# Mixture-of-experts stage of a vision-tower kernel: the last seven expert slots at 64 rows, with the routing arithmetic rewritten for them

## The reference, cut to what matters

```python
def _L0_ffn_ref(x, norm_scale, w_router, w_up, w_down):
    xn = rms_norm(x, norm_scale)
    scores = jnp.einsum('bsd,ed->bse', xn, w_router)
    _, ids = jax.lax.top_k(scores, TOP_K)                 # TOP_K = 2 of 8
    probs = jax.nn.softmax(scores, axis=-1)
    c = jnp.take_along_axis(probs, ids, axis=-1)
    h = jnp.einsum('bsd,ehd->bseh', xn, w_up)             # 256 -> 1408, every expert
    val, gate = jnp.split(h, 2, axis=-1)
    h = val * jax.nn.silu(gate)                           # 704
    y = jnp.einsum('bseh,edh->bsed', h, w_down)           # 704 -> 256
    yk = jnp.take_along_axis(y, ids[..., None], axis=2)
    out = jnp.sum(yk * c[..., None], axis=2)
    return out + skip
```

## Time and profile before

| | us |
|---|---|
| median of three executions (lowest, highest) | 1308.99 (1300.41, 1309.66) |
| the profiled execution | 1306.81 |
| its span from first to last instruction | 1305.2 |
| PE busy (share of the span) | 1173.4 (90%) |
| PE weight loads | 940.5 (72%) |
| DVE, ACT, POOL busy | 761.0, 577.0, 458.2 |
| routing: from DVE's first instruction of it to the first turning of rows on PE | 230.24 to 249.21 |
| the slots: from there to the end of the last down product | 249.21 to about 562.6 |

### The profile page before, as it was taken

One profiled execution on the slowest core, in us unless ns is written; L12 is line 12 of the kernel. 1 busy time (PEld: TensorE's weight loads), 2 busy tenths in 40 slices (PEclk: granted clock), 3 DMA queues, 4 the chain that ended last, 5 costly groups with the idle time before them and its releaser, 6 DMA issues. The chain is left out here.

```text
span 1305.2 us, 26300 instructions
## 1 busy us (share of the span) xinstructions
PE 1173.4 (90%) x9755; PEld 940.5 (72%) x9755; DVE 761.0 (58%) x1709; ACT 577.0 (44%) x1514; POOL 458.2 (35%) x630
## 2 busy tenths in 40 slices
PE   6999998498999999998799999995899999879975
PEld 4666667498999999984477777774777777657643
DVE  4666666511111212157899999974677777432687
ACT  3445453111122111127888787851344444335455
POOL 0111111233233333234488787851122122020556
PEclk9999999599999999999999999997999999889985
DMA  4111100599788888639500000002000050027611
GB/s 145 46 46 37 49 10 18 207 350 387 296 325 322 316 314 327 235 114 270 158 1 1 1 2 1 1 1 89 9 10 10 14 198 2 2 68 281 201 46 66
DMA packets 82719, 162.34 MB, mean 124 GB/s; under 512 B 42976, under 2 KB 61536, under 8 KB 76576
## 3 DMA queue, kind: packets, MB, share of 16 engines
q1 hardware_dynamic: 63776, 114.44, 25.6%
q0 software_dynamic: 10224, 44.05, 8.7%
q10 hardware_dynamic: 8592, 2.16, 0.8%
HBM read 134.28 MB, written 26.35 MB: 123 GB/s over the span
## 5 line engine op out<-in xcount | busy, mean ns | idle before, releaser
L936 PE MATMUL banks<-rowsT,w_up 128*128 128x128 f32 x1716 | 201.7, 278 | 0.0
L936 PEld LDWEIGHTS banks<-rowsT,w_up 128*128 128x128 f32 x1716 | 198.6, 195 | 0.1
L1486 PEld LDWEIGHTS banks<-chain_q,ident 128*128 128x128 f32 x992 | 120.5, 188 | 29.2 <-issue 29.2
L1476 PE MATMUL banks<-xT_d,ident 128*128 128x512 f32 x256 | 123.6, 605 | 7.2 <-POOL xT_d L1934 3.7
L1934 POOL TENSOR_TENSOR xT_d<-kb,ys 128x1024 f32<-128x1024 f32 x64 | 123.7, 1932 | 7.1 <-ACT ys L1611 5.8
L1486 PE MATMUL banks<-chain_q,ident 128*128 128x128 f32 x992 | 120.9, 273 | 0.0
L1627 ACT ACTIVATE banks<-banks,rate 128x256 f32<-128x256 f32 x252 | 98.5, 448 | 41.9 <-DVE made L1835 39.4
L1105 DVE TENSOR_TENSOR hT<-banks,silu 64x128 f32<-64x128 f32 x39 | 11.0, 283 | 167.8 <-ACT silu L993 167.8
L950 PE MATMUL banks<-w_down,hT 128*128 128x256 f32 x468 | 107.5, 379 | 0.6 <-DVE res L1115 0.6
L950 PEld LDWEIGHTS banks<-w_down,hT 128*128 128x128 f32 x468 | 85.9, 190 | 11.0 <-issue 1.0
L878 POOL DMA_DIRECT2D w_down<-in_down_w x39 | 22.2, 570 | 189.5 <-PE banks L950 181.3
(11 more groups left out here) (332 smaller groups left out, 2409.1 us busy)
## 6 DMA issues: line engine op xcount, KB each, us to landing
w_up<-in_up_w SPq DMA_DIRECT2D x39, 1408.0 KB, 6.1
w_down<-in_down_w POOLq DMA_DIRECT2D x39, 768.0 KB, 5.3
inter<-res_x SPq DMA_DIRECT2D x16, 512.0 KB, 3.4
back<-inter SPq DMA_DIRECT2D x15, 512.0 KB, 3.8
patches<-in_patches SPq DMA_DIRECT2D x16, 384.0 KB, 3.3
f<-in_f SPq DMA_DIRECT2D x6, 1024.0 KB, 11.6
ys<-token_rows SPq DMA_DIRECT2D x16, 256.0 KB, 2.8
xn_rows<-xn_all SPq DMA_DIRECT2D x16, 128.0 KB, 1.7
```

Source lines behind the costliest of these rows:

```text
L936: ins = pe.matmul(out[:, m * P:(m + 1) * P], w[:, c, m * P:(m + 1) * P], x[:, c, :], start=(c == 0), stop=(c == 1))
L1476: pe.matmul(S[t % 2][:, halves[h], :, :], ident[:, :], outer[t % 2][:, halves[h], :, :], start=(t == 0), stop=True, skip_group_check=True) ...
L1486: ins = pe.matmul(o_sum[n % 2].rearrange("p (n s) -> p n s", s=2), ident[:, :], products[:, n % 2, :, k, :], start=(k == 0), stop=(k == HD ...
```

## The change

Slots 0 to 31 (`FULLS`) keep 128 rows; slots 32 to 38 have 64 (`used_rows`). An expert gets whole slots for its rows, and a remainder of 1 to 64 rows gets one half slot; where more than 32 whole ones are wanted, the rest stand in two half slots each (`odd_at`, `jump`, `upper`). The number of slots, and of loads of `w_up` and `w_down`, stays 39.

In a half slot the turning, the up products, the copies, the SiLU values and the multiplications take 64 rows. Each of the six down products is split into two column halves of `w_down`, which write partitions 0 to 63 and 64 to 127 of the result bank (`Y_HALF`), and DVE copies the result in two pieces.

In the routing, `choose_slots` and `name_rows` get more small instructions on DVE. `choose_experts` moves from DVE to POOL and is written as a chain of 13 instructions; POOL also makes `named` for the pairs (`name_pairs`). The fourth lot of `row_hot` moves to ACT: eight squares of the distance to the row, then one ReLU of 1 minus it. Behind the naming products PE issues eight dummy products (`keep_warm`).

The core of the diff:

```diff
+FULLS = 2 * T
+USED = FULLS + E - 1
...
+    Y_HALF = [banks[q * TOK:(q + 1) * TOK, 6, 0:P] for q in range(2)]
+    def used_rows(j):
+        return P if j < FULLS else TOK
...
-        pool.wait_ge(sem("tile_at"), 1)
+        pool.wait_ge(sem("h_padded"), 2)
+        pool.wait_ge(const_in, 16 * len(const))
+        choose_experts(pool)
+        name_pairs(pool)
         fetch_down(0)
         pool.wait_ge(sem("source"), 1)
         gather(0)
...
-                    ins = pe.matmul(out[:, m * P:(m + 1) * P], w[:, c, m * P:(m + 1) * P], x[:, c, :],
+                    ins = pe.matmul(out[:, m * P:m * P + n], w[:, c, m * P:(m + 1) * P], x[:, c, 0:n],
...
+            if j < FULLS:
+                for c in range(HIDC):
+                    ins = pe.matmul(Y, hT[j % 2][:, c, :], w_down[j % DEEP][:, c, :], start=(c == 0), stop=(c == FULL))
+            else:
+                for c in range(HIDC):
+                    for q in range(2):
+                        ins = pe.matmul(Y_HALF[q], hT[j % 2][:, c, 0:TOK], w_down[j % DEEP][:, c, q * P:(q + 1) * P],
+                                        start=(c == 0), stop=(c == FULL), skip_group_check=True)
...
-            if i % LOT == 0:
+            if i == ACT_LOT * LOT:
+                pe.wait_ge(sem("act_row_hot"), 1)
+            elif i % LOT == 0:
                 pe.wait_ge(sem("row_hot"), i // LOT + 1)
...
+        keep_warm(pe, banks[:, 2, 0:P], ident[:, :], 8)
...
+        act.wait_ge(sem("row"), 1)
+        for i in range(LOT):
+            ins = act.activation(distance[:, i, :], const["row_no"][:, :], ACT.Square, scale=-1.0,
+                                 bias=row[:, ACT_LOT * LOT + i:ACT_LOT * LOT + i + 1])
+        ins.then_inc(sem("distance"), 1)
...
+        act.activation(row_hot[:, ACT_LOT * LOT:PAIRS, :], distance[:, :, :], ACT.Relu, scale=-1.0, bias=1.0
+                       ).then_inc(sem("act_row_hot"), 1)
...
+    def choose_experts(pool):
+        pool.wait_ge(sem("odd_at"), 1)
...
+    def name_pairs(pool):
+        pool.wait_ge(sem("slot_hot"), 1)
+        pool.tensor_tensor(named[:, 0, :, :], slot_hot[:, :, :], bcast(const["pair_start"][:, :], 2, USED), ALU.mult
+                           ).then_inc(sem("pair_named"), 1)
...
-        for i in range(4):
+        for i in range(ACT_LOT):
...
+                dve.tensor_copy(res[j % KEPT][0:TOK, 0:P], Y_HALF[0])
+                dve.tensor_copy(res[j % KEPT][0:TOK, P:D], Y_HALF[1]).then_inc(sem("y_copied"), 1)
```

More of the change, by code:

```diff
@@ L833, in expert_layer @@
     per_tile = sb("per_tile", [P, E, T])
-    cmp = sb("cmp", [P, E, T])
-    need, ends, first = (sb(n, [P, E]) for n in ("need", "ends", "first"))
+    cmp = sb("cmp", [P, E, 2 * T])
+    need, ends, starts = (sb(n, [P, 2, E]) for n in ("need", "ends", "starts"))
+    odd_first, odd_at, ends_at, jump, limit, base = (sb(n, [P, E]) for n in (
+        "odd_first", "odd_at", "ends_at", "jump", "limit", "base"))
+    whole, odds_from = sb("whole", [P, 1]), sb("odds_from", [P, 1])
+    parts = sb("parts", [P, 2, E])
+    over = sb("over", [P, T, E])
+    upper = sb("upper", [P, PAIRS])
     where = sb("where", [P, T, E])
@@ L884, in gather @@
                 pool.wait_ge(sem("rowsT_made"), j - ROWS + 1)
+            n = used_rows(j)
             pool.indirect_dma_start(
[L886 to L887 removed]
+                out=rows[j % ROWS][0:n, :], out_offset=None, in_=xn_rows,
+                in_offset=bass.IndirectOffsetOnAxis(ap=source[0:n, j:j + 1].bitcast(U32), axis=0)
             ).then_inc(sem(f"rows{j % ROWS}"), 16)
@@ L948, in down @@
                 pe.wait_ge(sem("y_copied"), j)
-            for c in range(HIDC):
-                ins = pe.matmul(Y, hT[j % 2][:, c, :], w_down[j % DEEP][:, c, :], start=(c == 0), stop=(c == FULL))
+            if j < FULLS:
[6 more added lines that the diff above has]
+                                        start=(c == 0), stop=(c == FULL), skip_group_check=True)
             ins.then_inc(sem("y_made"), 1)
@@ L1065, in name_rows @@
                                             op1=ALU.subtract))
+        tally.settle()
+        tally.mark(dve.tensor_scalar(upper[:, :], row[:, :], float(TOK), float(TOK), ALU.is_ge, ALU.mult))
+        tally.settle()
+        tally.mark(dve.scalar_tensor_tensor(out=upper[:, :], in0=slot_at[:, :], scalar=float(FULLS * P), in1=upper[:, :],
+                                            op0=ALU.is_ge, op1=ALU.mult))
+        tally.settle()
+        tally.mark(dve.tensor_tensor(slot_at[:, :], slot_at[:, :], upper[:, :], ALU.add))
+        dve.tensor_tensor(row[:, :], row[:, :], upper[:, :], ALU.subtract).then_inc(sem("row"), 1)
+        tally.settle()
         dve.tensor_tensor(slot_hot[:, :, :], bcast(const["slot_start"][:, :], 1, PAIRS), bcast(slot_at[:, :], 2, USED),
                           ALU.is_equal).then_inc(sem("slot_hot"), 1)
-        choose_experts(dve, tally)
-        dve.wait_ge(sem("slot_hot"), 1)
-        dve.tensor_tensor(named[:, 0, :, :], slot_hot[:, :, :], bcast(const["pair_start"][:, :], 2, USED), ALU.mult
-                          ).then_inc(sem("pair_named"), 1)
-        for i in range(4):
+        dve.wait_ge(sem("row"), 1)
+        for i in range(ACT_LOT):
             at = slice(i * LOT, (i + 1) * LOT)
@@ L2908, in laid_out_more @@
     keep = np.tile(np.arange(T) > 0, E)
+    halves = np.arange(USED) + np.minimum(np.arange(USED), FULLS)
     return {
@@ L2921, in laid_out_more @@
         "keep": line(keep),
-        "keep_e": line(np.ones(E)),
-        "full": line(P * np.arange(T)),
+        "keep_e": line(np.arange(2 * E) % E > 0),
+        "full": line(TOK * np.arange(2 * T)),
         "row_no": line(np.arange(P)),
-        "slot_start": line(P * np.arange(USED)),
+        "slot_start": line(TOK * halves),
         "pair_start": line(P * np.arange(2 * T)),
```

120 lines of the change are left out of this document (80 added, 40 removed).

## The result

The changed kernel takes 1315.32 us (median of 13 runs, 1308.43 to 1328.48), the kernel before 1308.99 (13 runs). The ratio is 1.0062, with an interval of 1.0035 to 1.0089: slower by 0.6%, some 8 us (5 to 12 by the interval; the two medians lie 6.3 us apart), where 1307.5 and no change were forecast. It lies 1.3 us above the range. One of the 13 executions, the one of 1328.48, fell in a slower state of the chip and isn't in the ratio. The profiled execution took 1313.19 us with a span of 1311.5, against 1305.2 before.

A forecast was written before the change was run, and what follows sets the result against it. PE, busy nine tenths of nearly every slice, was taken to set the pace. From 1306.81 us, + 6.3 for slot 0's rows reaching PE later and - 5.6 for seven half slots gave 1307.5 us, no change; range 1299 to 1314.

The forecast's parts named there:

- Half slots: Seven half slots on PE: down products fall from 2.59 to 1.5 us, 0.8 saved each, 5.6 in all; bounds 3.5 to 8.
- Up products saved nothing: Up products of half slots: loading the block sets the pace, not the moving columns, so 0 for 7 x 44 instructions.
- Rival C: Half slots: up products go by their moving columns, 56 ns for 112, 17.2 us less, 1290.3 us; chance 0.06.
- DVE's chain: Routing on DVE: twelve or so short instructions come in, so `slot_hot` starts 2.9 us later.
- POOL's prices: Routing on POOL: 13 instructions cost 6.5 us together, among them 0.55 for the scalar one of 624 elements.
- rival D: Routing: POOL at a dearer price, 2.6 us for the 624 elements, rows at PE 8.7 later, 1309.9 us; chance 0.15.
- POOL and DVE exclude one another: Routing: one engine waits out the other; `slot_hot` put off by 1.4 us, `pair_named` 3.6 us later than without waits.
- rival B: Routing: POOL's chain runs beside DVE's without waiting, rows at PE 2.5 us later, 1303.7 us; chance 0.25.
- The gather behind the loads: Slot 0's gather, 2.84 us from issue to PE before, takes 0.7 us more while `w_up` and `w_down` still load.
- The dummies win 0 ahead of up(1): Dummy products speed up(0) by 2.4 us, but up(1) waits for its `w_up` anyway: 0; bounds -1 to +2.4.
- The forecast is wrong if the stretch from slot 1 to slot 31 changes at all: Sign for the profile after: the full slots from 1 to 31 should take the same time as before.
- Rival E: Half slots: column halves run one after the other, down products take 2.7 us and save nothing, 1315.2 us; chance 0.06.

The follow-up runs named there:

- e3: The changed kernel with POOL issuing the gather ahead of the load of `w_down`; 1306.13 us, ratio 1.0004.
- e7: The changed kernel with up products of half slots moving 128 columns, gathers still late; 1311.4 us, ratio 1.0046.
- e4: The changed kernel with POOL repeating its subtraction, clip and four adds behind `named` while DVE is idle; one execution, 1327.34 us.
- e2: The changed kernel with experts chosen on DVE by one comparison and one sum, POOL keeping the pairs' names; 1316.85 us, ratio 1.0071.
- e6: The changed kernel with experts chosen on DVE and the gather ahead of the load of `w_down`; 1300.01 us, ratio 0.9953.
- e9: As e6, without the eight dummy products; 1300.01 us, ratio 0.9936.
- e8: The changed kernel with the gather first and six down products of 256 columns per half slot, not twelve column halves; 1311.28 us, ratio 1.0031.
- e10: As e6, with the wait for slot 0's rows put ahead of slot 2's `w_up` load, no longer slot 1's; 1302.32 us, ratio 0.9944.
- e11: As e10, without the eight dummy products; 1295.89 us, ratio 0.9914.

## Why the prediction failed

The sum was + 6.3 - 5.6 = + 0.7 us. The trace has + 10.1 up to up(1), - 1.0 from there to up(31), - 0.3 behind it: + 8.8. Of the 8.1 us that the forecast missed, the half slots are 5.3 and the routing up to up(1) is 3.8, less the 1.0 between. Either alone would have left the time inside the range. The top of the range was short as well: the routing's bound of 11, the slots' 3.5 and up(1)'s 2.4 add up to 1316.7, not 1314.

**Half slots, the term that failed.** "Seven save 5.6" was right as a price: undisturbed they save 6.5 (58.48 for 64.96), a slot 0.94 for the 0.8 forecast. The down products take 1.48 for 1.5; the change of form into the down products costs 0.15 for 0.1 (5.06 for 4.91 from up to down), and that into the turnings 0.04 for 0.2, which is the difference. The step that failed is that the saving was taken as a saving of time. I costed PE's work and never asked what a faster slot asks of the gather. Its room is 6.0 us in full slots (530.09 to 536.11) and falls by what a slot gets shorter, to 5.2 (539.30 to 544.53), and the gather took 6.6 to the turning. Then the clock fell behind the wait. Held against e3, the kernel after loses 6.2 us in the last slots, 1.4 of it with the wait and 4.8 with the clock. Neither was in the bounds of 3.5 to 8. e3 shows it, by mending the order of issue alone.

**Up products saved nothing, right**: 5.06 to 5.12 us for 44 with 64 columns, 5.18 with 128 (e7). Rival C is out. The page "TensorE: Matmul & The Clock Gate" of the Trainium skill (Back-to-back issue gap) has a table of isolated products by which they would halve, but says ahead of it that in a stream of loads and products both set the spacing. The trace agrees with the latter: each of these products has a new float32 block of 128 columns ahead of it, and 44 take the same time with 64 and with 128 moving columns.

**DVE's chain, right**: `slot_hot` starts 9.98 us into the routing for 6.11 before, + 3.87, of which 1.05 is `picked` held off by POOL. The 2.8 that remain were forecast as 2.9.

**POOL's prices, mis-sized.** "The scalar one 0.55" took 2.33, rival D's 2.6 nearly: the row of 256 elements at 3.7 ns each came nearer, and I had taken the one of 208 elements. Neither stands under the clip's operations, a maximum and a minimum: that of 208 multiplies and adds, that of 256 subtracts and multiplies. The 39-element steps with two constants were put at 0.3 and took 0.37 to 0.43. That is + 2.1 together; `pair_named` ends 20.2 us into the routing, where the forecast had 18.6 and D 21.0. The names end + 7.2 later for + 5.6.

**POOL and DVE exclude one another, right** (against rival B). The four adds take 5.32 us beside lots of `row_hot` and 2.17 alone (e4); `named` 3.09 beside them (e2) and 2.27 alone. In e2 the lots of `row_hot` beside it lasted 1.908 us on average, where they had 1.216 before. The rule of the Trainium skill cited from "SBUF — State Buffer" (Who interferes with whom) is borne out here by those pairs. It isn't by another one: POOL's clip, which reads and writes SBUF, runs from 240.14 to 242.47, and `slot_hot`, with two inputs in SBUF, starts at 241.82 and takes 1.46 us, as before (1.45). Four short DVE instructions with two such inputs (L1145 to L1154) lie inside the clip and take 0.18 to 0.19 us, as they do in e2 with POOL idle. In this trace the one-input clip holds nobody up.

**The gather behind the loads, mis-sized**: + 0.7 forecast, + 2.0 found (4.81 for 2.84). e2 gives back 2.86 with slot 0's `w_up` issued 8.9 us earlier on the stage's scale and its `w_down` 3.7. `w_up` has landed there before the gather is issued (16.06 and 20.82), and in the kernel after it hasn't (26.08 and 23.35); which speaks for what flew beside it. Rows at PE: + 9.2 for + 6.3, and D's + 8.7.

**The dummies win 0 ahead of up(1), right** in e6 and e9 (33.06, 32.85), but by another wait than the one named: slot 2's rows came first there (2.14 us of 2.39), `w_up` a little later. "The lower of the two clocks" for up(0) before was a part of it only: the clock granted from 251.0 to 258.4 us is 0.65. In the kernel after itself the dummies ended 2 us before the rows came, and up(0) ran at 0.75. The wait for `w_up` came (2.23 for "about 2.5"), and the clock at up(1) fell, which I had kept as a bound of + 2.4 and not in the sum; it cost 1.7 (6.80 for 5.12).

**"The forecast is wrong if the stretch from slot 1 to slot 31 changes at all"**: it changed by - 1.0. It got 1.7 from the slow up(1), and took back 2.7 in the slots behind it, 2.0 of it from shorter waits for rows: 3.8 us in slots 8 to 10, where before it was 5.8 in all (waits of 0.55 and 3.27 there and of 0.40 and 0.41 further on, and up(9) 1.17 longer).

Rival D had the routing right, and on top of it the half slots gave 0.3 for 5.6; 1309.9 + 5.3 is 1315.2, and the measured median 1315.3. That it comes so near is luck: the sum starts from an execution 2.2 us under the median, and the 0.9 us lost between the rows and up(1) is made up by the 1.0 won behind it. Rival E has that same number by a cause that isn't there: the column halves do run side by side, as the earlier trace rows had it and e8 shows by its absence.

## What to carry to other kernels

A saving per step shortens the room of every transfer that is issued a fixed number of steps ahead: before counting it, subtract it from the time between each issue and its use, and look for a queue in which an issue that waits for nothing stands behind one that waits (here, one swap of two calls was worth 7.2 us in the kernel before, and 6.2 in the half slots of the kernel after). A chain moved to an engine that is idle isn't free if that engine is dear per element and shares something with the one that it was taken from: 3.0 us on DVE were 11.8 on POOL, 3.2 of them spent waiting for DVE. Take the price from the row with the same operations and the dearer figure when two rows disagree.

## What the runs showed of the hardware

- POOL's TENSOR_SCALAR with a maximum and a minimum takes 2.30 us for 624 elements (3.7 ns each), alone and in company, a TENSOR_TENSOR of the same size 1.25.
- A short POOL tensor_tensor beside a series of long DVE ones is held up, and holds them up: 39 elements took 1.12 us for 0.26 alone (e4), and the lots beside the four adds 1.573 on average for 1.216; POOL's 1.29 us in turn stretched two DVE products from 0.49 to 1.54.
- The POOL clip (TENSOR_SCALAR) did neither: DVE's `slot_hot`, begun 0.65 us before it ended, took 1.46 us for 1.45.
- Half-size turnings and up products among whole down products cost too: in e3 the slots from 501.53 to 509.50 and on to 517.47 last 7.97 us where full ones take 7.72.
- The granted clock fell to 0.50 behind waits of 0.4 to 1.3 us among products of 64 moving columns (the kernel after, e2, e4), and up and down products then took 8.06 and 2.83 us for 5.12 and 1.53. With 128 moving columns waits of 0.99 (e7, one profile) and, in full slots, of up to 1.73 (after) and 2.43 (e2) left it at 1.00, while 2.27 (e7) and 3.27 (before) did not; and without waits products of 64 columns kept it at 1.00 in e3, e6, e9, e10 and e11.
